# DLRM tower: the first group of the first chunk takes its shifted rows from PSUM transposes, and layer 0 of the rest runs beside layer 1

## The reference

```python
def _cin_layer(X0, Xi, W, b):            # W: 128 x (39 * Fi)
    Wr = W.reshape(H, F0_, Fi)
    return jnp.einsum('hjk,bjd,bkd->bhd', Wr, X0, Xi) + b[None, :, None]
e = jnp.stack([tbl_0[ids[:, 0]], ..., tbl_38[ids[:, 38]]], axis=1)   # 512 x 39 x 16
Xi = X0 = e
for W, b in ((W0, b0), (W1, b1), (W2, b2)):
    Xi = _cin_layer(X0, Xi, W, b)
    res.append(Xi.sum(axis=2))
h = jnp.concatenate([jnp.concatenate(res, axis=1), dense_ctx], axis=1)   # 512 x 400
h = jnp.maximum(h @ W_top1 + b_top1, 0.0)
h = jnp.maximum(h @ W_top2 + b_top2, 0.0)
y = h @ W_top3
```

## Time and profile before

| | us |
|---|---|
| median of 3 runs | 705.97 |
| lowest and highest | 704.32, 708.51 |
| profiled execution | 708.72 |
| its span | 706.9 |
| TensorE busy | 666.6 (94%) |
| VectorE busy | 558.3 (79%) |
| ScalarE busy | 500.9 (71%) |
| GpSimd busy | 362.2 (51%) |

### The profile page before, as it was taken

The page is one execution under the profiler, slowest core; times in us unless marked ns, Lnnn a source line. Parts: engine busy times, 40 slices in busy tenths (PEclk is TensorE's granted clock), DMA queues, the critical chain, the costliest instruction groups (busy, mean ns, idle before and its releaser), DMA issues.

```text
span 706.9 us, 15108 instructions
## 1 busy us (share of the span) xinstructions
PE 666.6 (94%) x2978; PEld 475.0 (67%) x2978; DVE 558.3 (79%) x1211; ACT 500.9 (71%) x1629; POOL 362.2 (51%) x351
## 2 busy tenths in 40 slices
PE   0279999999999999999999999999999999999998
PEld 0137777777777777777777777777777777764443
DVE  0337889999989898999999999999998999995000
ACT  0327878788787878788878787878878787983002
POOL 6867774847565565656574747474753333000000
PEclk9999999999999999999999999999999999997999
DMA  6335423222221313031312222222222120001000
GB/s 212 92 105 179 147 51 85 50 70 63 71 63 48 85 18 104 15 100 34 90 45 84 49 84 50 84 50 71 63 71 60 46 67 4 1 17 60 0 1 0
DMA packets 28094, 45.73 MB, mean 65 GB/s; under 512 B 5968, under 2 KB 9424, under 8 KB 27817
## 3 DMA queue, kind: packets, MB, share of 16 engines
q1 hardware_dynamic: 20249, 39.06, 18.2%
q10 hardware_dynamic: 2704, 5.11, 2.9%
q0 software_dynamic: 5120, 1.32, 2.0%
HBM read 40.36 MB, written 5.11 MB: 64 GB/s over the span
## 4 chain that ended last, share of the span: by engine, by line
PE 88%; DVE 4%; issue 2%; DMA 2%; ACT 1%; POOL 0%; DVEq 0%; SPq 0%; ACTq 0%
PE acc L332 14%; PE ya L355 12%; PE ya L356 11%; PE ya L357 11%; PE yd L357 8%; PE yd L355 8%; PE yd L356 8%; PE yd L423 5%; PE misc L339 5%; PE misc L317 3%; DVE chain L466 2%; DMA x_rows<-x 1%; DVE x2t L481 1%; PE misc L324 1%; DMA tiles<-x_rows 1%
## 5 line engine op out<-in xcount | busy, mean ns | idle before, releaser
L581 ACT ACTIVATE prods<-ya,x0t 128x128 f32<-128x128 f32 x1472 | 446.8, 500 | 107.0 <-PE ya L357 105.4
L466 DVE SCALAR_TENSOR_TENSOR chain<-yd,x0t,chain 128x128 f32<-128x128 f32 x768 | 219.1, 343 | 19.6 <-PE yd L357 17.1
L355 PE MATMUL ya<-w1h,x1h 128*128 128x512 f32 (+1 forms) x384 | 207.1, 539 | 0.0
L202 POOL TENSOR_TENSOR prod<-tiles,x0a 120x512 f32<-120x512 f32 x105 | 136.9, 1305 | 104.5 <-PE acc L332 97.8
L262 POOL DMA_INDIRECT emb<-in_tables,rows x160 | 158.9, 993 | 38.7 <-issue 27.1
L356 PE MATMUL ya<-w1l,x1h 128*128 128x512 f32 (+1 forms) x384 | 148.2, 386 | 0.0
L357 PE MATMUL ya<-w1h,x1l 128*128 128x512 f32 (+1 forms) x384 | 147.6, 384 | 0.0
L481 DVE TENSOR_REDUCE x2t<-prods 128x128 f32<-128x1792 f32 x64 | 129.2, 2019 | 1.5 <-DVE chain L466 0.3
L332 PE MATMUL acc<-prod,w 120*128 120x512 f32 x224 | 116.1, 602 | 8.8 <-DVE prod L202 8.8
L481 DVE TENSOR_REDUCE prods<-prods 128x128 f32<-128x1536 f32 x64 | 111.7, 1745 | 0.0
L283 POOL TENSOR_TENSOR diag<-x0t,const 128x320 f32<-128x320 f32 x64 | 46.3, 723 | 121.4 <-PE misc L339 121.4
(11 more groups left out here) (68 smaller groups left out, 437.0 us busy)
## 6 DMA issues: line engine op xcount, KB each, us to landing
tiles<-x_rows SPq DMA_DIRECT2D x112, 240.0 KB, 3.4
w<-in_w SPq DMA_DIRECT2D x2, 2496.0 KB, 11.0
x_rows<-x ACTq DMA_DIRECT2D x16, 312.0 KB
x0a<-x_rows SPq DMA_DIRECT2D x48, 80.0 KB
emb<-in_tables,rows POOLq DMA_INDIRECT x160, 2.4
prods<-in_W_top SPq DMA_DIRECT2D x2, 512.0 KB, 4.6
gram<-in_w0ab SPq DMA_DIRECT2D x1, 840.0 KB, 6.5
x<-in_W_top SPq DMA_DIRECT2D x1, 256.0 KB, 2.6
```

Source lines behind the costliest of these rows:

```text
L202: engine.tensor_tensor(prod0[:, i % L0_PRODS, :], tiles[:, slot, :], x0a[:, :], ALU.mult).then_inc(prod0_ready, 1)
L355: pe.matmul(out, x1h[:, xs], w1h[:, cols], start=True, stop=False)
L466: dve.scalar_tensor_tensor(out, product, x, run if step else b1[:, :], ALU.mult, ALU.add).then_inc(yd_used, 1)
L581: mm = act.activation(prods[:, :, slot_of(q) + i], ya[(NA * g + k) % YA][:, i * H:(i + 1) * H], ACT.Copy, scale=turned(c)[:, g * F1 + j:g ...
```

## The change

The start of chunk 0 is rearranged, and some places in the loop and the tail move with it.

- **First group.** Layer 0 of group 0 of chunk 0 no longer uses `scratch`. ScalarE evacuates group 0 of the layout first. TensorE transposes it, ScalarE copies it out of PSUM repeated (`x0w_a`, three times with 40 rows; `x0w`, four times 39), TensorE transposes windows of it back (one for the factor, seven for the shifted tiles, into `yd[1]` and `ya`), VectorE multiplies out of PSUM in four instructions (`first_products`), and seven matmuls of 128 columns follow.
- **Rest of chunk 0.** The other three groups (384 columns) take their tiles through `scratch` as before, now written from SP's queue. Their products (`layer0_cols`) are made and multiplied between the layer 1 blocks of group 0 (`L0_REST`), on VectorE and TensorE. The layout of chunk 1 comes after block 6 of that group and its turning after block 9.
- **W1.** It is loaded in three parts, and ScalarE splits it ahead of everything but a bias.
- **GpSimd.** One gather of chunk 1, not three, stands ahead of the first widening. Of chunk 2 six gathers stand ahead of the first product of chunk 1, the other four between its products, and then `widen(2)`; the gathers of chunk 3 stand between the last products and behind them.
- **Loop.** `LAY_AFTER` and `X0T_AFTER` move from groups 0 and 1 to 1 and 2 (in chunk 0 to 2 and 3).
- **Tail.** `hidden1_early(3)` runs ahead of the last gram, and parts 3 and 5 use other PSUM banks.

```diff
-LAY_AFTER, X0T_AFTER, G_AFTER = (0, 1), (1, 1), 6
+L0_REST = {3: (0,), 4: (1,), 5: (2,), 6: (3,), 7: (4,), 8: (5, 6)}
+LAY_1, X0T_1 = 6, 9
+LAY_AFTER, X0T_AFTER, G_AFTER = (1, 1), (2, 1), 6
+def lay_group(prev):
+    return 0 if prev else 1
...
+            cols = layer0_cols(x)
+            engine.tensor_tensor(prod0[:, i % L0_PRODS, cols], tiles[:, slot, cols], x0a[:, cols],
...
-        hid, hid2 = (acc0, ya[0], ya[1], misc), (yd[1], ya[2])
+        hid, hid2 = (acc0, ya[0], ya[1], ya[2]), (yd[1], ya[3])
...
-            sp.dma_start(w2[:, :, :], a["w1"]).then_inc(w1_in, 16)
+            for i in range(W1_PARTS):
+                sp.dma_start(w1_raw[:, w1_part(i)], a["w1"].rearrange("p j h -> p (j h)")[:, w1_part(i)]
+                             ).then_inc(w1_in[i], 16)
+            sp.wait_ge(x0_ready, 1)
+            sp.dma_start(chunk_rows(0).rearrange("(u j) n -> j u n", u=COPIES),
+                         x0[0:F, :].rearrange("p (u n) -> p u n", u=1).to_broadcast([F, COPIES, COLS]),
+                         ).then_inc(scratch_in, 16)
...
-            gather(1, range(3))
+            gather(1, range(1))
...
             widen(0)
-            gather(1, range(3, FO))
+            gather(1, range(1, FO))
             gather(2, range(2))
             widen(1)
-            gather(2, range(2, FO))
-            for c in range(CHUNKS):
+            gather(2, range(2, 6))
+            multiply0(pool, 1, 0)
+            gather(2, range(6, 8))
+            multiply0(pool, 1, 1)
+            block_diagonal(0, 0)
+            gather(2, range(8, FO))
+            multiply0(pool, 1, 2)
+            multiply0(pool, 1, 3)
+            widen(2)
+            block_diagonal(0, 1)
+            multiply0(pool, 1, 4)
+            gather(3, range(1))
+            multiply0(pool, 1, 5)
+            gather(3, range(1, 2))
+            multiply0(pool, 1, 6)
+            block_diagonal(0, 2)
+            gather(3, range(2, 6))
+            block_diagonal(0, 3)
+            gather(3, range(6, FO))
+            for c in range(1, CHUNKS):
...
+            def first_group():
+                for q in range(BLOCKS):
+                    layer1_block(0, 0, q)
+                    for i in L0_REST.get(q, ()):
+                        if i == 0:
+                            pe.wait_ge(first_x1, 1)
+                        layer0(0, i)
+                    if q == LAY_1:
+                        pe.wait_ge(x0t_ready, 1)
+                        lay_out(1)
+                    if q == X0T_1:
+                        pe.wait_ge(x0_ready, 2)
+                        turn_x0(1)
...
             lay_out(0)
+            pe.wait_ge(first_x0, 1)
+            pe.transpose(yd[0][:, 0:FP], x0[:, FIRST], const[0:FP, C_ID:C_ID + FP]).then_inc(first_turned, 1)
+            pe.wait_ge(first_x0w, 1)
+            pe.transpose(yd[1][0:K0, 0:P], x0w_a, identity).then_inc(first_picked, 1)
+            pe.wait_ge(first_x0w, 2)
+            for i in range(T0):
+                pe.transpose(ya[i // 2][0:K0, i % 2 * P:(i % 2 + 1) * P], x0w[:, 3 * i:3 * i + K0],
+                             identity).then_inc(first_picked, 1)
             pe.wait_ge(x0_ready, 1)
             turn_x0(0)
             pe.wait_ge(w0_ready, 1)
             for i in range(T0):
-                layer0(0, i)
-            pe.wait_ge(x0t_ready, 1)
-            lay_out(1)
-            pe.wait_ge(x0_ready, 2)
-            turn_x0(1)
-            pe.wait_ge(w1_split, W1_PARTS)
+                pe.wait_ge(first_prod, i // 2 + 1)
+                pe.matmul(acc0[:, FIRST], w0[:, i, :], first_prods[:, i, :],
+                          start=(i == 0), stop=(i == T0 - 1)).then_inc(first_l0, 1)
+            pe.wait_ge(first_x1l, 1)
+            first_group()
...
             hidden1_early(1)
+            pe.wait_ge(ya_used, NA * GROUPS * CHUNKS)
             hidden1_early(2)
+            hidden1_early(3)
             gram_group(GROUPS * CHUNKS - 1, GROUPS - 1)
...
-            hidden1_early(3)
...
+            def first_products(i, n):
+                dve.wait_ge(first_picked, i + n + 1)
+                dve.tensor_tensor(first_prods[:, i:i + n, :],
+                                  ya[i // 2][0:K0, 0:n * P].rearrange("p (i n) -> p i n", i=n),
+                                  first_a.rearrange("p (i n) -> p i n", i=1).to_broadcast([K0, n, P]),
+                                  ALU.mult).then_inc(first_prod, 1)
+            def first_group():
+                multiply_add(0, 0, 1)
+                multiply0(dve, 0, 0)
+                multiply_add(0, 0, 3)
+                multiply0(dve, 0, 1)
+                multiply0(dve, 0, 2)
+                multiply0(dve, 0, 3)
+                multiply_add(0, 0, 6)
+                sum_half(0, 0, 0)
+                multiply0(dve, 0, 4)
+                multiply_add(0, 0, 8)
+                multiply0(dve, 0, 5)
+                multiply0(dve, 0, 6)
+                split_x1(0, slice(P, (GROUPS - 1) * P), x1h_front, x1_front)
...
+            for q in range(BLOCKS):
+                if OWNERS[q] == "A":
+                    multiply(0, 0, q)
+                if q == LAY_1 + 1:
+                    evacuate_layout(1)
             evacuate_x1(0)
-            evacuate_layout(1)
+            split_back(0)
             evacuate_x0t(1)
```

More of the change, by code:

```diff
@@ L155, in build @@
         yd = [ps(f"yd{i}") for i in range(YD)]
-        ids_in, const_in, w0_in, w1_in, w2_in = (sem(n) for n in ("ids_in", "const_in", "w0_in", "w1_in", "w2_in"))
+        ids_in, const_in, w0_in, w2_in = (sem(n) for n in ("ids_in", "const_in", "w0_in", "w2_in"))
+        w1_in = [sem(f"w1_in{i}") for i in range(W1_PARTS)]
+        first_x0, first_turned, first_x0w = sem("first_x0"), sem("first_turned"), sem("first_x0w")
+        first_picked, first_a_ready, first_prod = sem("first_picked"), sem("first_a_ready"), sem("first_prod")
+        first_l0, first_x1, first_x1h, first_x1l = sem("first_l0"), sem("first_x1"), sem("first_x1h"), sem("first_x1l")
         bias_in, mlp0_in, mlp_in, out_done = sem("bias_in"), sem("mlp0_in"), sem("mlp_in"), sem("out_done")
@@ L181, in build @@
         tail_mm, tail_act = sem("tail_mm"), sem("tail_act")
+        FIRST, REST = slice(0, P), slice(P, COLS)
         FRONT, BACK = slice(0, (GROUPS - 1) * P), slice((GROUPS - 1) * P, COLS)
@@ L190, in turned, with layer0_cols @@
             return x0t[:, bass.ds(c & (XT - 1), 1), :].rearrange("p c n -> p (c n)")
+        w1_raw = w2[:, :, :].rearrange("p j h -> p (j h)")
         def w1_part(i):
             return slice(i * F // W1_PARTS * H, (i + 1) * F // W1_PARTS * H)
+        def layer0_cols(x):
+            return REST if isinstance(x, int) and x == 0 else slice(0, COLS)
         def multiply0(engine, x, i):
@@ L359, in chunk @@
             def chunk(c, prev, nxt, lay):
-                l0_after = L0_AFTER if prev else L0_AFTER_0
-                for g in range(GROUPS):
-                    if g == 0:
+                l0_after, late = L0_AFTER if prev else L0_AFTER_0, lay_group(prev)
+                lay_after = LAY_AFTER[0] + late, LAY_AFTER[1]
+                x0t_after = X0T_AFTER[0] + late, X0T_AFTER[1]
+                for g in range(0 if prev else 1, GROUPS):
+                    if g == (0 if prev else 1):
                         pe.wait_ge(x1_front, c + 1)
@@ L379, in chunk @@
                             turn_x0(c + 2)
-                        if q == G_AFTER and (g or prev):
-                            if lay and g < 2:
-                                pe.wait_ge((x0_ready, x0t_ready)[g], c + 3)
-                            gram_group(GROUPS * c + g - 1, (g - 1) % GROUPS)
+                        if q == G_AFTER:
+                            if not prev and g == 1:
+                                pe.wait_ge(x0t_ready, 2)
+                            if lay and g == lay_after[0]:
+                                pe.wait_ge(x0_ready, c + 3)
+                            if lay and g == x0t_after[0]:
+                                pe.wait_ge(x0t_ready, c + 3)
+                            gram_group(GROUPS * c + g - 1, (g - 1) % GROUPS)
@@ L557, in evacuate_x1 @@
                 wait_done(act, z_sums, c)
-                act.activation(x1[:, :], acc0[:, :], ACT.Identity, bias=bias[:, 0:1]).then_inc(x1_ready, 1)
+                cols = layer0_cols(c)
+                front = slice(cols.start, FRONT.stop)
+                act.activation(x1[:, cols], acc0[:, cols], ACT.Identity, bias=bias[:, 0:1]).then_inc(x1_ready, 1)
                 act.wait_ge(x1_ready, c + 1)
-                act.activation(x1h[:, FRONT], x1[:, FRONT], ACT.Copy).then_inc(x1h_front, 1)
+                act.activation(x1h[:, front], x1[:, front], ACT.Copy).then_inc(x1h_front, 1)
             def split_back(c):
@@ L585, in chunk @@
             def chunk(c, prev, nxt, lay):
-                split_back(c)
-                for g in range(GROUPS):
+                if prev:
+                    split_back(c)
```

(29 more changed lines are left out.)

42 lines of the change are left out of this document (26 added, 16 removed).

## The result

The changed kernel takes 710.31 us (median of 4 runs, 709.49 to 711.19) against 705.32 (4 runs) of the kernel before: ratio 1.0071, interval 1.005 to 1.0092. It is slower by 5 us, where I forecast 704.6 and a range up to 708.5. The profiled execution took 709.49, with a span of 707.7.

The account below looks back on a forecast made before the run. TensorE was taken as the bound, busy 37.30 us per chunk, with GpSimd limiting the earlier start. Start -3.2 and tail +1.85 gave -1.35, so the median 705.97 became 704.6 us; range 700 to 708.5.

Parts of the forecast that it names:

- What costs nothing: Loop: layout moves from group 0 to 1, turning from 1 to 2, at no cost, with 20 us left for GpSimd.
- my 3.2 us: Start: TensorE takes the first product of chunk 2 at 87.4 instead of 90.6, gaining 3.2 us.
- the tail's 1.85: Tail: the fourth early pair, moved ahead, costs 3.83 us where it cost 2.0: +1.85; zero if the clock stays up.
- The sum's first term: Start of chunk 0: first widening at about 20.6 us against 20.81, with gathers slowed by the W1 subtractions.
- rival (c): Start: TensorE stays at its lower level, S is 39.9, the start loses 1.8 us, total 709.6; chance 0.1.
- S: Chunk 0: start of the first layer-0 product of the other three groups, forecast at 34.9 us.
- M: GpSimd's first product of chunk 1, forecast at S+17.75 = 52.65 us, against 53.61 before.
- that mark: TensorE's first product of chunk 2: 90.6 us for the kernel before, adjusted for the later layout; forecast 87.4.
- (a): Start: gathers not slowed, widening at 18.5, 5.9 us gained; 700.1 if the tail's clock stays up; chance 0.2.
- (b): Chunk 0: GpSimd is not the bound, TensorE sets the pace at 86.2, total 703.4; chance 0.1.

Follow-up runs that it names:

- warm-up experiment: Sixteen matmuls of constants ahead of the first layout, added to the held-back split with the tail of the kernel before: 700.47 us against 704.89 for the kernel before.
- held-back split: Changed kernel with the loop put back, second and third W1 subtractions held until the first widening is done: 702.63 us against 704.95 for the kernel before.
- the tail alone: Kernel before with only the tail's edits (fourth early pair ahead of the last gram, other PSUM banks): 707.03 us against 704.95.
- the loop put back: Changed kernel with the loop's layout and turning back at groups 0 and 1: 703.64 us against 704.95 for the kernel before.
- the start alone: Changed kernel with both loop and tail as in the kernel before: 704.35 us against 704.76 for the kernel before.

## Why the prediction was wrong

**The step that failed** is "What costs nothing": the layout's move from group 0 to 1 in the loop. I checked the room of the transfers and GpSimd behind it, and that VectorE's long group 1 would profit. I did not ask what the 1.34 us in group 0 had been hiding. I had VectorE's 34 us of 37.3 only as an average. At the chunk's border, where two splits and two sums begin within 5 us, there was no slack. It had been hiding VectorE's lateness, and without it block 3 waits: the runs put 0.46 us on each chunk. Of the 5.7 us from chunk 2 to 13 in the profile, 0.63 is in chunk 2 and the rest 0.46 to 0.48 each. The part put back is worth 6.0 us, and alone in the kernel before it costs the same 0.46. Without it the forecast's range would have held the time (703.64, 1.3 under its kernel before, where I had 1.35). That match would have been luck: the start gained far less than my 3.2 us and the tail's 1.85 was not there, and the two errors cancel.

**The start: right in kind, mis-sized.** The sum's first term was too small. Three gathers beside the three subtractions lost 3.3 us together (2.49 + 2.06 + 1.57 less 3 x 0.94), where I had scaled 2.06 us to 1.9: the widening was at 21.70, not 20.6. From there layer 0 of the group began 0.5 us later than I had it, since the seven transposes took 1.70 us (28.92 against my 27.3, with 1.1 from the widening). It took 3.35 us (forecast 3.5), and the first block was at 33.40 (32.0). Then the four blocks took 4.6 us and not 2.8, since the passes kept the spacing of the lower level, 0.43 us, until 36.6: half of rival (c). (The profile's clock column reads 1.00 there; the durations show the level.) So S was 38.17, not 34.9, just past the point (38.1) that I gave for a loss. From there the chain held: M is S+17.2 (forecast 17.75), the first product of chunk 2 M+34.6 (34.8), and its wait 0.87. The gain at that mark was 0.6 us, not 3.2, and 0.4 in the medians. The warm-up experiment shows that one term at fault was the clock, the held-back split that the other was the subtractions.

**The tail.** The term of +1.85 is the price if the clock falls ahead of the pair. For the pair itself it was 0 in both profiles of the changed kernel and in that of the tail alone, and 2 where the clock fell early. Three comparisons of kernels that differ in the tail alone give -0.9 (the loop put back against the start alone, on two chips), -0.1 and +2.1 us, and none tells it from zero.

**The rivals.** (a) was out with the long gathers. (b) was out: TensorE waited for GpSimd at chunk 2, as forecast. (c), with 0.1, came half true, but its start alone would have explained under 2 us of the loss. The mechanism that decided stood in none of them.

## What to carry to other kernels

Before work is moved away from a place in a loop that shows no wait, look at what finishes behind it on the other engines at that very place: filler on the bounding engine may be what hides their lateness. A turn that lacks the filler, often the last ones, shows in the old trace what its absence costs; and a busy share of 91% over the whole turn says nothing about the border between two. A cost of half a microsecond in the loop outweighs a start that begins layer 1 twelve microseconds sooner. And when a start is moved into the time of another load, price the engines' effect on each other and the clock level at which the moved work will run by rows from the start, not by rows of the loop.

## What the runs showed of the hardware

- An indirect gather on GpSimd takes 0.94 us alone and 1.57 to 2.49 beside a VectorE subtraction of two SBUF tensors (1.89 us long); the loss was 1.1 us per subtraction, more than the 0.69 of the kernel before. Why it differs is not shown.
- TensorE's granted clock fell to 0.50 in the tail at 642.7, 644.0, 645.4, 649.4, 650.4 and 654.3 in six profiles, the last of them the changed kernel's second, and not in its first. In five of the six TensorE had no idle time in the pairs ahead of the fall, in the one at 644.0 it had 0.24 us just before. Of the kernels with nine or more runs, each has them spread over 4 to 9 us.
- At the start, work on constants ahead of the first layout brought it from 2.31 to 1.41 us and 14 passes of 128 columns from 3.35 to 1.80. The transposes in between (seven in 0.98 us instead of 1.70) and the gaps around them did not end the full level.
